# Products of the identity in front of TensorE's waits in the two stages that prepare attention heads

## The reference, cut to what matters

```
h = h + _L0_attn_ref(_layernorm(h), qkv_w, qkv_b, proj_w, proj_b, rpb_table)   # 8 heads of 8, windowed bias
...
h = _rmsnorm(x, ln1_w); q, k, v = h @ wq.T, h @ wk.T, h @ wv.T                 # 4 query heads, 2 key heads of 16
q = q * cos + _rotate_half(q) * sin; k = k * cos + _rotate_half(k) * sin
scores = q @ k.T / sqrt(HD); causal mask; softmax; @ v
```

## Time and profile before

| | |
|---|---|
| median of 3 runs | 2583.45 us (2580.28 to 2589.42) |
| profiled execution | 2582.66 us, span 2580.9 us |
| mean granted TensorE clock | 0.901 |
| busy | PE 90%, DVE 71%, ACT 55%, POOL 16% of the span |
| chain that ended last | PE 75%, DVE 10%, ACT 5% |

### The profile page before, as it was taken

One profiled execution on the slowest core, in us unless ns is written; L12 is line 12 of the kernel. 1 busy time (PEld: TensorE's weight loads), 2 busy tenths in 40 slices (PEclk: granted clock), 3 DMA queues, 4 the chain that ended last, 5 costly groups with the idle time before them and its releaser, 6 DMA issues.

```text
span 2580.9 us, 55201 instructions
## 1 busy us (share of the span) xinstructions
PE 2334.8 (90%) x20147; PEld 1072.7 (42%) x20178; DVE 1837.4 (71%) x4732; ACT 1422.1 (55%) x2576; POOL 424.9 (16%) x502
## 2 busy tenths in 40 slices
PE   8987679999999999999689998987799999699998
PEld 3326523333333333332544444576544444533333
DVE  4566768888888888884367776659767775366775
ACT  2116727777777777777045553327666667144443
POOL 2002200000000000000623332132100110411110
PEclk9997769999999999999589997655699999589999
DMA  3113620101101010030755552245612222734422
GB/s 96 25 31 102 219 66 26 39 26 36 29 26 39 26 38 27 26 65 6 164 148 154 158 146 61 65 116 155 239 45 67 69 93 44 160 75 100 97 61 60
DMA packets 254351, 208.23 MB, mean 81 GB/s; under 512 B 191571, under 2 KB 197892, under 8 KB 253828
## 3 DMA queue, kind: packets, MB, share of 16 engines
q1 hardware_dynamic: 240914, 176.43, 25.8%
q0 software_dynamic: 10368, 19.06, 2.6%
q10 hardware_dynamic: 2808, 9.22, 1.5%
HBM read 138.78 MB, written 65.90 MB: 79 GB/s over the span
## 4 chain that ended last, share of the span: by engine, by line
PE 75%; DVE 10%; ACT 5%; issue 4%; POOL 3%; DMA 2%; SPq 1%; DVEq 0%; ACTq 0%; POOLq 0%
PE ps L1580 11%; PE ps L1486 7%; PE ps L1551 6%; PE ps L2813 3%; PE ps L2293 3%; PE ps L2800 3%; PE ps L2309 3%; PE ps L1191 3%; PE ps L1165 3%; PE ps L2824 3%; PE ps L364 3%; PE ps L1576 3%; PE ps L376 2%; PE ps L1103 2%; PE ps L1106 1%
## 5 line engine op out<-in xcount | busy, mean ns | idle before, releaser
L1666 DVE TENSOR_REDUCE att_mpart<-ps 128x1 f32<-128x512 f32 x1024 | 633.9, 684 | 56.3 <-PE ps L1486 51.2
L1624 ACT ACTIVATE att_p<-ps 128x704 f32<-128x704 f32 x768 | 546.5, 760 | 215.5 <-PE ps L1551 208.3
L1580 PE MATMUL ps<-att_p,att_v 128*9 128x352 f32 x3072 | 301.3, 463 | 0.1
L1486 PE MATMUL ps<-att_kT,att_qT 64*128 64x512 bf16 x1024 | 281.2, 386 | 21.0 <-DMA att_qz<-qt_d 8.4
L1551 PE MATMUL ps<-att_qT,att_kT 64*128 64x352 bf16 x1536 | 251.5, 317 | 7.3 <-ACT att_p L1624 6.9
L1280 DVE TENSOR_REDUCE cau_mpart<-ps 128x1 f32<-128x512 f32 (+5 forms) x384 | 193.1, 552 | 81.1 <-PE ps L1106 67.9
L1247 ACT ACTIVATE cau_p<-ps 128x704 f32<-128x704 f32 (+6 forms) x272 | 171.6, 660 | 82.3 <-PE ps L1165 49.7
L1457 POOL DMA_DIRECT2D o_d<-att_o x128 | 64.3, 509 | 840.7 <-ACT att_o L1607 840.5
L1551 PEld LDWEIGHTS ps<-att_qT,att_kT 64*128 64x128 bf16 x1536 | 82.0, 93 | 273.5 <-issue 263.9
L2367 ACT ACTIVATE mo_g<-ps 128x768 f32<-128x768 f32 x176 | 133.2, 807 | 105.3 <-PE ps L2293 105.3
L2881 ACT ACTIVATE mo_act<-ps 128x512 f32<-128x512 f32 (+1 forms) x216 | 109.7, 559 | 145.2 <-PE ps L2800 145.1
(11 more groups left out here) (412 smaller groups left out, 3894.8 us busy)
## 6 DMA issues: line engine op xcount, KB each, us to landing
mo_gate<-wg_d SPq DMA_DIRECT2D x176, 192.0 KB, 4.1
mo_gate<-wg_d SPq DMA_DIRECT2D x64, 256.0 KB, 5.2
qt_d<-pre_qT SPq DMA_DIRECT2D x8, 1056.0 KB, 4.3
kt_d<-pre_kT SPq DMA_DIRECT2D x8, 1056.0 KB, 7.2
att_kT<-kt_d SPq DMA_DIRECT2D x32, 264.0 KB, 2.8
att_qT<-qt_d SPq DMA_DIRECT2D x32, 264.0 KB, 3.0
cqt_d<-cpr_qT SPq DMA_DIRECT2D x8, 1056.0 KB, 4.4
cau_qT<-cqt_d SPq DMA_DIRECT2D x16, 528.0 KB, 4.0
```

Of the source, the lines that this page charges most:

```text
L1486: mm = pe.matmul(ps[:, bank, :], qT[half(s), u, j * P:(j + 1) * P], kT[half(s), u, c * BANK:(c + 1) * BANK], start=True, stop=not near)
L1580: mm = pe.matmul(ps[32 * cg:32 * cg + DV, 7, 0:TH], v[:, u, i, s, :], p[:, r, s, :], start=i < 2, stop=i == FULL - 1)
L1624: e = act.activation(p[:, n % PRING, :, :], ps[:, bank:bank + 2, 0:TH], ACT.Exp)
L1666: red = dve.tensor_reduce(mpart[:, j, s, c:c + 1], ps[:, bank, :], AX.X, ALU.max)
```

## The change

A helper issues n matrix products of the bf16 identity with itself, read four times over (512 columns). Their result goes to a PSUM bank that the next instructions overwrite, and nothing reads it. Calls stand in turn (3), heads (2) and stacks (4) of both stages, in `heads_prep`'s stacks only where b + 2 < B: 64 products in `heads_prep` and 72 in `causal_prep`. In heads the wait for xT, and in `stacks_turn` the wait for low_made, now come after the waits for the bank and after the products.

```diff
+def keep_busy(pe, const, bank, n):
+    eye = const["eye16"]
+    for _ in range(n):
+        pe.matmul(bank.rearrange("p (a b) -> p a b", b=P), eye[:, :], eye[:, :].unsqueeze(1).broadcast_to([P, 4, P]),
+                  start=True, stop=True)
...
@@ heads_prep, turn
                 at_least(pe, kt_cp, (b - 2) * 4)
+                keep_busy(pe, const, ps[:, 0, :], 3)
                 pe.wait_ge(xn_made, b + 1)
@@ heads_prep, heads
                 for m in range(NB):
-                    pe.wait_ge(xt_cp, b * 3 + m // 2 + 1)
                     at_least(pe, rest_made, (b - 1) * 2 * NB + 2 * m + 2 if b else 0)
                     if m == NB - 1:
                         at_least(pe, vt_made, b)
+                    if m == 0:
+                        keep_busy(pe, const, ps[:, 3, :], 2)
+                    pe.wait_ge(xt_cp, b * 3 + m // 2 + 1)
@@ heads_prep, stacks
                 at_least(pe, xt_cp, min(b + 3, B) * 3)
+                if b + 2 < B:
+                    keep_busy(pe, const, ps[:, 0, :], 4)
                 pe.wait_ge(low_made, (b + 1) * 2 * NB)
@@ causal_prep, rows_turn
                     if t == 0:
+                        keep_busy(pe, const, ps[:, XT, :], 3)
                         pe.wait_ge(S["xn_made"], b + 1)
@@ causal_prep, heads
                 at_least(pe, S["vt_made"], b * 4)
+                keep_busy(pe, const, ps[:, QKV, :], 2)
@@ causal_prep, stacks_turn
-                pe.wait_ge(S["low_made"], b * 2 + 2)
                 for c, (kind, i, _) in enumerate(TURNS):
                     n = b * NTURN + c
                     if n >= 3:
                         pe.wait_ge(*copied(n - 3))
+                    if c == 0:
+                        keep_busy(pe, const, ps[:, TURN + n % 3, :], 4)
+                        pe.wait_ge(S["low_made"], b * 2 + 2)
```

## The result

The changed kernel takes 2594.28 us (median of 11 runs) against 2584.63 us (11 runs of the kernel before beside them): ratio 1.005, 95% interval 1.0033 to 1.0067, slower by a little more than the 0.3% that the prediction takes as the least that can be told from no change. The profiled execution took 2593.85 us (before: 2582.66), its span 2592.1 us. The forecast was 2594.

What follows compares the result with a forecast made beforehand. No engine was taken as full; chains between batches bound both stages, ACT's in heads_prep. Terms -0.8 + 2.5 + 8.5 + 0.5 = +10.7 us, from the median 2583.45, gave 2594 us, range 2578 to 2607.

Steps and rivals of the forecast that it cites:

- The sum: Whole kernel: -0.8 for heads_prep, +2.5 and +8.5 + 0.5 for causal_prep, +10.7 us in all, 2594 us.
- The price of a product: Both stages: one 512-column product costs as much as four 128-column transposes, 0.43 us at low clock, 0.22 at high.
- Causal_prep, steady: Causal_prep's loop: products behind the wait delay the stacks, partly regained; +1.7 us a batch, +8.5 over five batches.
- Causal_prep, start: Causal_prep's start: three products before the first turn, +1.0, and four before the first stacks, +1.5; +2.5 us.
- The last part of the stage: Causal_prep's batch with heads alone: two and four products added, a faster first three sets gained; +0.5 us.
- Heads_prep, steady: Heads_prep's loop: four products exposed at +0.88, faster blocks and turns give time back; -1.6 us over the stage.
- Heads_prep, start: Heads_prep's start: eight products add 3.4 us, faster heads and turns give back up to 3.6; 0, between -1.2 and +3.4.
- Rival one: Causal_prep: the two products at once bring heads to the high clock; total -4 us, 2579.5; chance 0.32.
- Rival two: The products don't count for the clock: 2637 us, on the slower side; its chance isn't in the text given.
- Rival three: Both stages: clock high at each first set, all products hidden except four; -11 us, 2572; chance 0.10.

Runs made afterwards that it cites:

- heads_prep alone: The changed kernel without its three calls in causal_prep, so products in heads_prep only: 2588.61 us against 2585.46 for the kernel before, ratio 1.0018.

## Why the prediction was right

- **The sum.** +10.7 forecast on the profiled execution, +11.2 measured. The mechanism and the stage were right: products behind the wait ahead of heads, at the low clock, added to the way to the stacks. That the number is so near is in part luck. The two stages together are 13.3 us longer and not 10.7 (causal_prep +12.9 for +11.5, heads_prep +0.4 for -0.8), and code that isn't changed took 2.2 us less, 1.2 ahead of heads_prep and 1.0 between the stages.
- **The price of a product.** 0.22 us at the high clock (four in 0.88 and 0.87) and 0.42 at the low one (three in 1.26), against 0.22 and 0.43. Comparing columns with 128-column transposes was enough.
- **Causal_prep, steady: the term that was low.** +8.5 forecast for five batches; from the starts 1765.92 to 1832.56 before and 1765.42 to 1842.83 after it is +10.8, 2.15 a batch and not 1.7. Stacks start 7.3 to 10.0 us behind a batch's start (mean 8.86; 6.9 to 10.4 forecast), and 1.3 comes back in the mean, 7.94 to 6.62 (1.25 forecast). The low clock holds over all of heads in three of the five batches (0.50), over part of it in two (means 0.75 and 0.69), and over the three products in all (0.50). The reason given for it was wrong: the idle gap did not grow to 3 us, it is 2.47. Faster stacks ahead of the gap don't decide it either, as the batches above show; when the clock falls stays open.
- **Causal_prep, start.** +2.5 forecast. The first stacks come 24.08 us after the stage's first TensorE row and not 22.11: +2.0. These stacks then take 0.6 less to the next batch, a term that the sum doesn't have. The last part of the stage: +0.9 for 0.5.
- **Heads_prep, steady.** -1.6 forecast, -1.3 measured over the six batches from the first stacks to the seventh (86.81 to 85.56 us): +0.8 in the first and -2.1 in the other five. Three batches are 13.95 to 14.0 us for the 13.8 foreseen; the four were taken at 0.88 and cost 0.65. What the sum lacked is the tail, 19.1 us before and 20.4 now from the seventh stacks to the end: of the last stacks six sets of eight run at the low clock (0.80 to 0.86 us from start to start, 318.67 to 323.74) and not three.
- **Heads_prep, start.** 0 forecast between -1.2 and +3.4, and +0.8 in front of the first stacks. From the stage's first TensorE row to the end of the second turn it is 1.4 less, and the first stacks still come 0.5 later. The lower bound isn't worked out from its terms: 3.4 less what is given back, up to 3.6, is -0.2, and with all eight products at the high clock (8 x 0.22) it would be -1.8. The argument that work with no gap had raised the clock elsewhere isn't in the rows either: between the turn of 260.25 and the transposes of 262.98, over which the clock rose (0.50 over 264 to 265, 0.90 over the next us), TensorE was idle for 0.63 us, and turn, heads and turn in one piece, 9.8 us from 195.74, left it low (0.50 over 203.44 to 205.50). Nor is the start as steady as it was taken to be: in the kernel with causal_prep's products in the gap, heads(0) took 3.81 us with no product in heads_prep at all.
- **Rival one, the clock stays high** (2579.5): heads at 4.21 us, and at no less than 2.9 in any of the five batches, says no for the change. With the products in the gap the same mechanism gives 12.98 us a batch, so what it foretold was right for another place.
- **Rival two, the products don't count** (2637): out. All 136 are in the changed kernel's trace, 64 and 72, so none was dropped. Heads(0) is at 3.09 to 3.63 us behind five products and a turn in six kernels; behind a turn alone it is at 6.01 in six of the seven kernels without products there and at 3.81 in the seventh, and behind 32-column products at 6.11. With the nine in the gap heads is at 2.24 us each time, at a granted clock of 1.00 in the batch shown above. So products of the identity did raise and hold the clock in these kernels. Transposes raised it too. The last stacks of heads_prep before the change are transposes alone, behind 4.97 us without work, and their sets of eight go from 1.01 to 0.61 us (granted clock 0.50 over 320.51 to 321.51, 1.00 over 323.51 to 324.51):

```profile
320.51 1.01 PE L769 MATMUL ps<-eye,pre_qs 128*128 128x128 bf16 x8 [4.97 <-DVE pre_ks L880]
...
323.58 0.61 PE L769 MATMUL ps<-eye,pre_qs 128*128 128x128 bf16 x8
```

- **Rival three** (2572): the four aren't hidden (0.88 us in front of the stacks, at a cost of 0.65 a batch), as said against it.

## What to carry to other kernels

Work that is only there for the clock belongs in the idle time itself, ahead of the wait that ends it, with operands and a bank that are free by then. Behind the wait it lengthens what follows, and here it came too late for the work next behind it (in causal_prep heads took 4.21 us in three of five batches, and 2.24 with the products in the gap). In causal_prep nine products behind the waits cost 2.2 us a batch, and 16 in the gaps gave 0.4 to 0.7. Before adding any, ask what the clock can give at all: for each stretch at the low clock, who is the next to be waited for.

## What the runs showed that was not expected

- The mean granted clock rose by 0.12 in the stage that got 12.9 us longer. It rose where extra work was done (0.62 to 0.74), and was no measure of gain.
- The same 18 instructions of heads in causal_prep take anything from 2.4 to 4.1 us to the next row's start in kernels that have no product there, behind idle gaps of 2.2 to 2.7 us, and 2.87 to 4.14 in the changed one. A single batch is a poor measure of what the clock costs.
- Code that no kernel changed differs between profiles by more than the gains here: the long middle between the two stages took 1394.6 to 1408.4 us, heads_prep without products 136.1 to 140.6. Why wasn't tried. Gains of 2 us were read from starts in the stage, and only the ratios over several runs tell of the whole; heads_prep alone, at 1.0018 with an interval of 1.0001 to 1.0036 and no longer stage, shows that even they can stand clear of 1 by that much without a cause that was found.
